# Splitting the expert matrices in the list steps instead of once ahead of them, in a two-layer mixture kernel

## What is computed

```python
base_out   = einsum('bsi,oi->bso', x, base_w) + base_b
res_hidden = einsum('bsi,ri->bsr', x, A)                 # 64 ranks for a row
logits     = einsum('bsi,ei->bse', x, router_w)          # 16 experts
topw, topi = top_k(softmax(logits), 2)                   # two experts for a row
delta      = einsum('bse,bsr,eor->bso', combine, res_hidden, B)   # B: 16 x 1024 x 64
return base_out + delta * SCALING
```

## Time and profile before

| | before |
|---|---|
| median of 3 runs | 1200.79 us (1199.48 to 1203.69) |
| the profiled execution: time | 1200.46 us |
| the profiled execution: span of the core | 1198.5 us |
| TensorE busy | 1171.6 us (98%) |
| ScalarE busy | 767.6 us (64%) |
| VectorE busy | 706.4 us (59%) |
| GpSimd busy | 297.5 us (25%) |
| DMA | 267.15 MB, mean 223 GB/s |

### The profile page before, as it was taken

The page is one execution under the profiler, slowest core; times in us unless marked ns, Lnnn a source line. Parts: engine busy times, 40 slices in busy tenths (PEclk is TensorE's granted clock), DMA queues, the critical chain, the costliest instruction groups (busy, mean ns, idle before and its releaser), DMA issues.

```text
span 1198.5 us, 22055 instructions
## 1 busy us (share of the span) xinstructions
PE 1171.6 (98%) x6783; PEld 1034.3 (86%) x6783; DVE 706.4 (59%) x1985; ACT 767.6 (64%) x1746; POOL 297.5 (25%) x315
## 2 busy tenths in 40 slices
PE   6999999999999999999999999999999999999998
PEld 6999999999899999898787787787788888888887
DVE  6677778777465655557764444454445555555552
ACT  5566667666586776864667767767645665755751
POOL 4111733323222223234312112111131222222200
PEclk9999999999999999999999999999999999999999
DMA  9566566775999999979699999999875455455410
GB/s 333 185 241 258 191 225 229 285 268 165 253 319 327 311 322 311 325 269 242 127 245 304 268 293 311 281 292 299 269 165 118 99 123 110 118 123 118 110 53 36
DMA packets 84698, 267.15 MB, mean 223 GB/s; under 512 B 23248, under 2 KB 27472, under 8 KB 77360
## 3 DMA queue, kind: packets, MB, share of 16 engines
q1 hardware_dynamic: 72608, 230.12, 58.4%
q0 software_dynamic: 11600, 36.06, 17.0%
q10 hardware_dynamic: 432, 0.30, 0.1%
HBM read 154.24 MB, written 112.20 MB: 222 GB/s over the span
## 4 chain that ended last, share of the span: by engine, by line
PE 41%; DMA 7%; SPq 1%; issue 1%; DVE 1%; ACT 1%; POOL 0%; ACTq 0%; POOLq 0%; DVEq 0%
PE z L1461 12%; PE z L1462 12%; PE z L1463 12%; DMA ht<-hs_dram 3%; DMA xin<-zs_dram,gpos 2%; DMA xin<-x_dram 1%; PE c L1461 1%; PE c L1463 1%; PE c L1462 1%; PE c L1528 1%; PE prep L1725 1%; DMA x<-zs_dram,gpos 1%; DVE xb L1433 1%; PE c L1532 1%; PE c L1530 1%
## 5 line engine op out<-in xcount | busy, mean ns | idle before, releaser
L754 ACT ACTIVATE moved<-mid 32x256 f32<-32x256 f32 x944 | 392.2, 415 | 139.0 <-DVE mid L1023 114.6
L1461 PE MATMUL z<-w_1h,yh 128*128 128x384 f32 (+1 forms) x512 | 190.0, 371 | 0.0
L1461 PE MATMUL z<-w_0h,yh 128*128 128x384 f32 (+1 forms) x512 | 187.4, 366 | 0.2 <-DVE xb L1433 0.2
L1463 PE MATMUL z<-w_1l,yh 128*128 128x384 f32 (+1 forms) x512 | 185.8, 363 | 0.0
L1463 PE MATMUL z<-w_0l,yh 128*128 128x384 f32 (+1 forms) x512 | 185.8, 363 | 0.0
L1462 PE MATMUL z<-w_1h,yl 128*128 128x512 f32 (+1 forms) x504 | 183.0, 363 | 0.0
L1462 PE MATMUL z<-w_0h,yl 128*128 128x512 f32 (+1 forms) x504 | 182.8, 363 | 0.0
L669 POOL TENSOR_TENSOR carrier<-ones_col 128x1 f32<-128x1 f32 x96 | 25.5, 266 | 539.1 <-DVE den L1117 131.8
L1461 PE MATMUL z<-w_2h,yh 128*128 128x336 f32 (+1 forms) x512 | 152.9, 299 | 2.1 <-DVE yl L1031 2.1
L1463 PE MATMUL z<-w_2l,yh 128*128 128x336 f32 (+1 forms) x512 | 152.5, 298 | 0.0
L1462 PE MATMUL z<-w_2h,yl 128*128 128x252 f32 (+1 forms) x504 | 149.9, 297 | 0.0
(11 more groups left out here) (217 smaller groups left out, 2587.8 us busy)
## 6 DMA issues: line engine op xcount, KB each, us to landing
bd<-bd_dram SPq DMA_DIRECT2D x96, 512.0 KB, 9.0
zs_dram<-zt SPq DMA_DIRECT2D x96, 512.0 KB, 10.2
hs_dram<-zt SPq DMA_DIRECT2D x34, 512.0 KB, 6.6
x8raw<-in_x_dram SPq DMA_DIRECT2D x32, 516.0 KB, 4.4
xin<-in_x_dram SPq DMA_DIRECT2D x32, 512.0 KB, 6.9
x_dram<-xb SPq DMA_DIRECT2D x32, 512.0 KB, 5.2
out_dram<-xb SPq DMA_DIRECT2D x32, 512.0 KB, 4.7
bd_dram<-bd SPq DMA_DIRECT2D x8, 1024.0 KB, 6.5
```

The lines of the kernel that those rows point to most:

```text
L754: return nc.scalar.activation(o, i_, ACT.Copy)
L1461: T.matmul(o, ah, wh, start=start, stop=False, **kw)
L1463: return T.matmul(o, ah, wl, start=False, stop=stop, **kw)
```

## The change

The copy `bd_dram` and the eight split steps are taken out. `load_bd` fetches the matrix of one expert as it is in the input, 256 KB, into half of the partitions of `bdraw[j]`. When both halves of a pair are there, ScalarE copies them to `bdh[j]` (`bd_high`, 128x1024) and VectorE subtracts (`bd_low`, 128x1024) into `bdl[j]`, which lies over `bdraw[j]`. `listed_pair` waits for `bd_lo`, not for the load. All of it happens twice in each of the 24 list steps.

```diff
-                sp.dma_start(bd[v // 2][ranks(v), :, :].bitcast(F32), bd_of[e]).then_inc(bd_in[v], 16)
+                sp.dma_start(bdraw[v // 2][ranks(v), :], b0_in_order[e]).then_inc(bd_in[v], 16)
...
-            def b_high(i, w):
...
+            def bd_high(s, j):
+
+                for v in (2 * j, 2 * j + 1):
+                    act.wait_ge(bd_in[v], 16 * s + 16)
+                copy(bdh[j][:, :], bdraw[j][:, :]).then_inc(bd_hi, 1)
...
                 if lists:
+                    bd_high(s, 1)
                     outputs(s, 0, cp, first=first_list)
                     outputs(s, 1, tp, first=first_list)
...
                 if turn is not None:
+                    bd_high(turn, 0)
                     ht_high(turn, first=at(turn, 0))
...
-            def b_low(t, w):
...
+            def bd_low(s, j):
+                dve.wait_ge(bd_hi, 2 * s + j + 1)
+                V.tensor_tensor(bdl[j][:, :], bdraw[j][:, :], bdh[j][:, :], ALU.subtract).then_inc(bd_lo, 1)
...
             def listed_pair(s, j):
 
                 pe.wait_ge(hl_ready, s + 1)
-                for v in (2 * j, 2 * j + 1):
-                    pe.wait_ge(bd_in[v], 16 * s + 16)
+                pe.wait_ge(bd_lo, 2 * s + j + 1)
```

More of the change, by code:

```diff
@@ L169, in build @@
         moved = sb(ctx, "moved", [P, L])
[L170 to L174, removed]
+        bdh, bdl, bdraw = zip(*(split_pair(ctx, f"bd{j}", [2 * R0, L]) for j in range(PER // 2)))
         ht = [sb(ctx, f"ht{j}", [P, 2 * R0]) for j in range(PER // 2)]
@@ L279, in build @@
         w0_lo = [sem(f"w0_lo{b}") for b in range(3)]
-        b_in = [sem(f"b_in{w}") for w in range(2)]
-        bd_out = sem("bd_out")
-        b_hi, b_lo = sem("b_hi"), sem("b_lo")
+        bd_hi, bd_lo = sem("bd_hi"), sem("bd_lo")
         cond_in, mlp_in, mixw_in, bias0_in = sem("cond_in"), sem("mlp_in"), sem("mixw_in"), sem("bias0_in")
@@ L494, in _, with step0 @@
             load_x(0, 1)
-            def step0(i, u, first=False, lists=None, more=True, start=False, clear=None, split=None):
+            def step0(i, u, first=False, lists=None, more=True, start=False, clear=None):
                 t = 2 * i + u
@@ L871, in mixed_out, with step0 @@
                     nc.scalar.activation(o, v, ACT.Identity, bias=mbrow[:, :]).then_inc(a1.c_out[b], 1)
-            def step0(t, u, first=False, split=None, w1_piece=None, lists=False, first_list=False, turn=None):
+            def step0(t, u, first=False, w1_piece=None, lists=False, first_list=False, turn=None):
                 s = t - S0_LISTS
@@ L908, in _ @@
                 step0(t, t % 2, first=t == 0)
-            for u in range(2):
-                step0(4 + u, u, split=(2, u))
-            with act.Fori(3, 6) as i:
+            with act.Fori(2, 6) as i:
                 for u in range(2):
-                    step0(2 * i + u, u, split=(i, u))
+                    step0(2 * i + u, u)
             step0(12, 0)
@@ L955, in step1 @@
                     w1_high(1, w1_pieces(1)[0:2])
+                if lists:
+                    bd_high(s, 0)
                 exps(a1, t)
@@ L1275, in residual, with step0 @@
                 V.tensor_tensor(o, z[b][:, 0:w.stop - w.start], o, ALU.add).then_inc(a0.z_out[b], 1)
-            def step0(i, u, w, first=False, split=False, w1_piece=None, tables=False, places=False, turn=None):
+            def step0(i, u, w, first=False, w1_piece=None, tables=False, places=False, lists=False, turn=None):
                 t = 2 * i + u
@@ L1296, in step0 @@
                 residual(i, u, 2)
+                if lists:
+                    bd_low(t - S0_LISTS, 1)
                 if tables:
@@ L1319, in step0 @@
                 if turn is not None:
+                    bd_low(turn, 0)
                     ht_low(turn)
@@ L1326, in _ @@
             for t in range(4, HELD):
[L1327 to L1328 removed]
+                step0(t // 2, t % 2, 0)
+            with dve.Fori(HELD // 2, 7) as i:
                 for u in range(2):
[L1330 to L1332 removed]
+                    step0(i, u, 0)
             step0(7, 0, 0, w1_piece=0)
@@ L1381, in step1 @@
             def step1(i, v, tiles=None, first=False, last=False, late=False, before_late=False, tables=False, places=False,
-                      turn=None):
+                      lists=False, turn=None):
                 t, u = 4 * i + v, v % 2
+                s = t - S1_LISTS + WS
+                if lists:
+                    bd_low(s, 0)
                 if late:
@@ L1403, in step1 @@
                     turn_rows(a1, tiles)
+                    if lists:
+                        bd_low(s, 1)
                 dve.wait_ge(a1.hT_hi, t + 1)
```

67 lines of the change are left out of this document (20 added, 47 removed).

## The result

| | before | after |
|---|---|---|
| median (4 runs each, one chip) | 1202.17 us (1199.48 to 1203.69) | 1221.43 us (1219.72 to 1223.51) |
| ratio after / before | | 1.0153, 95% interval 1.0125 to 1.0181 |
| span of the profiled execution | 1198.5 us | 1219.7 us |
| TensorE busy | 1171.6 us | 1174.1 us |
| ScalarE / VectorE busy | 767.6 / 706.4 us | 802.5 / 753.1 us |

A forecast was written before the change was run, and what follows sets the result against it. TensorE, busy 225.00 of 225.00 us in the first wave's list steps, was taken as the bound. Terms -1.0 - 2.6 + 19.7 + 0.5 = +16.6 on 1200.46 us gave 1217 us; 8-in-10 range 1200 to 1228.

The forecast's parts named there:

- The 12 waits of pair 1: First layer's list steps: GpSimd's earlier add holds VectorE ahead of bd_low, TensorE waits 1.6 us each, 19.7 us together.
- The queue: List steps: with 1 MB of some 5.8 MB gone per step, the DMA share falls from 0.98 to about 0.81.
- `ht` in the second layer: Second layer: halved matrix loads bring four late ht loads forward, 0 to -2.6 us, taken as -2.6.
- `x8l`: Three waits for the low part of the convolution's input, 2.5 us together: 0 to -2.5 us, taken as -1.0.
- The first list step: First list step: pair 0's loads land near 306, conv_out ends some 2 us late; 0.5 us added.
- The second layer at nothing: Second layer's 12 steps: two added copies and two subtractions each fit into three idle times, costing nothing.
- ScalarE and VectorE have just enough slack: First layer's list steps: added copies and subtractions alone just fit, using all slack; conv 0 to 0.4 us late.
- Rival 1: List steps: queue stays slow, store takes over 7.3 us, add falls behind bd_low; 1198 to 1202, say 1200; chance 0.19.
- Rival 4: List steps: new waits also lower TensorE's clock, conv 1.3 us longer each step, 16 us on top: 1233; chance 0.09.
- Rival 5: List steps: matrices land late and hold ScalarE, 1 to 2 us a step; chance 0.56 together with the forecast.

The follow-up runs named there:

- half_loads_only: The kernel before, with list-step matrix loads fetching only the high half, the third product reading the high part, and no copies added: 1197.04 us, ratio 0.9961.
- pool_after_low: The changed kernel, with GpSimd's bias add in the first wave's list steps waiting for pair 1's bd_low: 1204.71 us, ratio 1.0019.
- store_late: The changed kernel, with a 1 MB device-memory copy issued just ahead of the xb store in the first wave's list steps: 1203.03 us, ratio 0.9990.
- short_add: The changed kernel, with GpSimd's bias add cut from 1024 to 64 columns for tiles 18 to 31: 1200.70 us, ratio 0.9970.
- queue_filled: The changed kernel, with a 256 KB copy within device memory issued behind every matrix load: 1219.00 us, ratio 1.0141.
- early_split: The changed kernel, with the first wave's splits of both pairs moved forward, high parts behind ht_high, low parts behind conv_out: 1198.66 us, ratio 0.9972.

## Why the prediction was right

The forecast was 1217 us against 1221.43 measured; the medians put the change at +19.3 us where the sum had +16.6, and the two profiled spans at +21.2. The main term and its mechanism were right; some of the small terms were wrong, and those errors in part cancel. Point by point:

- **The 12 waits of pair 1**, put at 1.6 us each, 19.7 together: 19.3 us in 12, an average of 1.61. That the medians also differ by 19.3 us is chance, as the account of the spans below shows. The chain was as worked out, from the landed store over the add, `w`, and the first `residual` to `bd_low`. The single waits scatter more than the 1.3 to 2.3 us I gave, from 0.55 to 2.38, since the store's landing varies: in the twelve steps it is 4.6 to 6.6 us from the store to the add, against the 5.5 taken. I had the wait at 1.3 us or more wherever the add falls; with an add 4.6 to 5.2 us behind its store it is 0.55 to 0.84. That it matters little which operation is hit was right, with `w`, the one-hot and `bd_low` hit eight, three and one times.
- **The queue.** I had the DMA share at 0.81; it is 0.73. The sum made the share proportional to the bytes of a step but not to the step's own length, which grew by 9%: 0.81 x 18.88 / 20.60 = 0.74. In the kernels whose tile stayed at its old length, with no traffic added, the share is 0.78 to 0.80, beside the 0.81 for that length.
- **`ht` in the second layer**, -2.6 us: gone. The one `ht` wait left is in the first list step, as said. half_loads_only has none in the second layer either, which ties it to the loads.
- **`x8l`**, taken as -1.0: wrong, 3.2 us in place of 2.5. All of them, before and after, lie ahead of 300 us. The three old ones, at 98, 161 and 191 us, stay within 0.2 us of what they were although the split steps beside them are gone, and the fourth, 0.5 us, comes at 222 us, behind their place. I had given the split steps a part in them on no row that tied the two together.
- **The first list step**, +0.5: right in kind, too small in size, and already within the 19.3. Pair 1 starts 3.62 us later than before (320.01 against 316.39). 2.38 of it is the wait, and 1.2 us is older than the step, since TensorE ends the wait for the first `ht` at 303.17 in place of 302.02 and then takes 8.4 us to pair 0 in both. Within the 2.38 is what the late `conv_out` costs: where the add does not hold VectorE, this step still loses 0.75 us (pool_after_low), 1.07 (store_late) or 1.25 and 1.22 (short_add). ScalarE sits waiting there for the first two matrices:

```profile
307.32 1.06 ACT L725 ACTIVATE bd0h<-bd0raw 128x1024 fp32r<-128x1024 f32 x1 [7.63 <-DMA bd0raw<-in_b_dram]
```

- **The second layer at nothing**: right but for one `zt` wait of 0.6 us.
- **The sum of it** in the spans, which differ by 21.2 us: waits for `bd1l` +19.3, `zt` +0.6, `x8l` +0.7, `x1l` behind the wave +0.6, `ht` -2.7, and +0.3 in small ones, together +18.8; the rest is TensorE's busy time, 1174.1 against 1171.6 us, +2.5. The sum had nothing for that last term.
- **ScalarE and VectorE have just enough slack** for the copies: shown by pool_after_low, short_add and store_late, which keep all of them and lie at 1.0019, 0.9970 and 0.9990. Rival 1 was this case, and it is what the changed kernel would be with a slow store; store_late made it by hand.
- **Rival 4**, the clock: once. Behind the wait of 2.38 us the granted clock is 0.56 and 0.59, mostly the level of 1.2 GHz, from 320 to 324 us; it costs 1.7 us (the eight microseconds from 318 have a mean of 0.79). Behind the other eleven, up to 2.05 us, the stretch shows 1.00. As a price on every step it fell, but those 1.7 us are most of the 2.5 that the forecast lacked.
- **Rival 5**: in the tile shown ScalarE never sat waiting for a matrix; 256 KB land in 3.5 us. It did in the first list step (7.63 us, above), and in queue_filled, where copies delay the loads.

## What to carry to other kernels

An engine off the critical path has a phase as well as a load. Before taking traffic out of a full queue, look at what starts when its transfers land, and which operations of the busy engines stand at that moment; and put a new operation that TensorE waits for ahead of the place where another engine can hold its queue, even where the sums of work say that it fits. Here twelve subtractions in a bad place, 9.5 us behind the store in the tile shown, cost 1.5%. With the same ones 1.2 us behind it, and pair 0's out of the way of `conv_out`, the kernel gains 0.3%.

## What the runs showed of the hardware

- **The hold of VectorE by GpSimd** in the twelve steps of the changed kernel: `w` (128x2, 0.23 us alone) took up to 2.44 us, the one-hot (0.37 alone) 2.44 to 2.59, the subtraction (1.22 alone) 2.65. Not every operation with an SBUF input is held: in store_late the transpose of `moved` into `mid`, from SBUF to SBUF, started at 418.53 under the add of 417.47 and took 1.42 us, as it does with no add beside it. It works the other way too: GpSimd's one-column `carrier`, 0.19 us in the tile of early_split, took 1.10 us when it began 0.17 us after a subtraction. The Trainium skill, page SBUF — State Buffer, section Who interferes with whom, says that the first to start has the port for the whole instruction; the rows agree, in both directions. In the changed kernel, GpSimd and VectorE:

```profile
411.75 1.21 DVE L1107 TENSOR_TENSOR bd0l<-bd0raw,bd0h 128x1024 fp32r<-128x1024 f32 x1
...
411.92 1.10 POOL L640 TENSOR_TENSOR carrier<-ones_col 128x1 f32<-128x1 f32 x1 [11.30 <-DVE den L1088]
```

- **The landing time of one store against the load of the queue.** I had not expected it so steep. The same 512 KB store took, as median from issue to landing in the list steps, 5.6 us at a DMA share of 0.73, 5.9 to 6.5 at 0.78 to 0.80, 8.2 at 0.86, 8.4 at 0.90 and 10.8 at 0.98. Where the added traffic stands on the queue matters as well: the load of `x8raw`, 516 KB, took 8.1 us in queue_filled at 0.86, but 5.2 in store_late at 0.90, where the copy is issued behind it.
- **The first list step** differs among kernels whose edits don't touch its loads: the `ht` wait there was 1.7 us in short_add and 4.2 in pool_after_low. Up to 2.5 us of a difference between two of these kernels lie in this; the cause stays open.
- **The clock after an idle time** does not follow the length of that time alone. It fell behind waits of 2.18 us (pool_after_low, 0.68 and 0.50 from 564 to 568 us) and 2.38 us (the changed kernel), and did not fall behind one of 2.79 us (early_split, 1.00 from 302 to 310 us). No run here shows what decides.
